# First batch of a four-stage transformer kernel: norms ahead of the weights' scaling, a second issuing queue for 12 of the head tiles' transfers

## The reference

```python
x = x + attn0(layernorm(x), W_kv, g_kv, W_kdec, W_vdec, W_q, W_qdec, W_krope, W_qrope, W_o)
# in attn0, for 16 heads
kv_c = rmsnorm(x @ W_kv) * g_kv          # 32 wide
q_c = x @ W_q                            # 64 wide
k = [kv_c @ W_kdec (8 a head), rope(x @ W_krope) (32 a head)]
q = [q_c @ W_qdec (8 a head), rope(q_c @ W_qrope) (32 a head)]
v = kv_c @ W_vdec
out = (softmax(causal(q k^T * scale)) v) @ W_o
```

## Time and profile before

| what | us |
|---|---|
| median of 3 runs | 1621.32 |
| lowest and highest run | 1618.19, 1621.41 |
| span of the profiled execution, first to last instruction | 1581.6 |
| median less span | 39.7 |

### The profile page before, as it was taken

The page is one execution under the profiler, slowest core; times in us unless marked ns, Lnnn a source line. Parts: engine busy times, 40 slices in busy tenths (PEclk is TensorE's granted clock), DMA queues, the critical chain, the costliest instruction groups (busy, mean ns, idle before and its releaser), DMA issues.

```text
span 1581.6 us, 37199 instructions
## 1 busy us (share of the span) xinstructions
PE 1288.0 (81%) x13212; PEld 843.4 (53%) x13212; DVE 1160.2 (73%) x3814; ACT 728.0 (46%) x1523; POOL 690.9 (44%) x1004
## 2 busy tenths in 40 slices
PE   4479899888899888989995799938998898666891
PEld 2244544445454454545544566627776776556780
DVE  4578787896988969888764554428889998973556
ACT  1145456555555555555560133424545444215773
POOL 3023232233332333324231122347878788764664
PEclk9689999999999999999995899968879678658996
DMA  3675726556175561745606111102111112032335
GB/s 104 88 113 78 116 34 105 78 92 111 26 116 79 93 104 26 122 79 92 101 9 225 38 34 33 40 22 83 44 43 44 50 50 71 21 118 77 99 92 169
DMA packets 73863, 123.19 MB, mean 78 GB/s; under 512 B 17518, under 2 KB 46067, under 8 KB 72784
## 3 DMA queue, kind: packets, MB, share of 16 engines
q1 hardware_dynamic: 64960, 106.74, 35.5%
q0 software_dynamic: 7616, 13.59, 2.6%
q10 hardware_dynamic: 1104, 0.48, 0.1%
HBM read 30.40 MB, written 17.60 MB: 30 GB/s over the span
## 4 chain that ended last, share of the span: by engine, by line
PE 39%; DVE 30%; POOL 10%; issue 8%; DMA 5%; SPq 4%; ACT 3%; DVEq 1%; POOLq 0%; ACTq 0%
DVE first L780 5%; PE A L594 5%; PE S L1034 5%; PE S L577 4%; DVE S L783 4%; PE S L566 4%; POOL xq L1357 3%; SPq L500 3%; DVE tA L759 2%; PE A L1046 2%; PE S L558 2%; DVE tB L760 2%; PE A L1996 2%; DMA Qp<-mT 2%; PE S L179 2%
## 5 line engine op out<-in xcount | busy, mean ns | idle before, releaser
L671 ACT ACTIVATE P<-S 128x512 f32<-128x512 f32 (+3 forms) x768 | 333.1, 491 | 281.5 <-PE S L577 277.2
L854 POOL TENSOR_SCALAR_AFFINE_SELECT P<-P 128x256 f32<-128x256 f32 (+1 forms) x256 | 116.8, 460 | 384.9 <-ACT P L671 384.7
L566 PE MATMUL S<-Kp,Qp 120*128 120x512 f32 (+3 forms) x768 | 251.5, 396 | 36.0 <-DMA Kp<-rck 18.6
L577 PE MATMUL S<-Qp,Kp 121*128 121x512 f32 (+3 forms) x768 | 251.6, 391 | 35.4 <-DVE tB L760 9.8
L783 DVE CUSTOM_DVE_ANT_0 S<-S,later 128x512 f32<-128x512 f32 (+3 forms) x512 | 239.2, 514 | 39.4 <-PE S L566 38.8
L566 PEld LDWEIGHTS S<-Kp,Qp 120*128 120x128 f32 x768 | 133.5, 195 | 168.7 <-issue 75.5
L780 DVE TENSOR_REDUCE first<-S 128x1 f32<-128x512 f32 x256 | 164.5, 684 | 49.5 <-PE S L566 49.2
L577 PEld LDWEIGHTS S<-Qp,Kp 121*128 121x128 f32 x768 | 138.2, 191 | 112.4 <-issue 24.0
L594 PE MATMUL A<-P,V 128*9 128x512 f32 (+3 forms) x1536 | 175.3, 505 | 5.0 <-POOL P L854 5.0
L2133 POOL DMA_INDIRECT yq<-yq,id x71 | 69.4, 978 | 46.2 <-DVE yq L2096 22.5
L1780 POOL TENSOR_TENSOR prod<-qf,kT 128x128 f32<-128x128 f32 x160 | 72.8, 488 | 34.7 <-ACT qf L1615 21.7
(11 more groups left out here) (335 smaller groups left out, 2696.2 us busy)
## 6 DMA issues: line engine op xcount, KB each, us to landing
Qp<-rcq SPq DMA_DIRECT2D x64, 256.0 KB
Kp<-rck SPq DMA_DIRECT2D x64, 256.0 KB
Qp<-rcq SPq DMA_DIRECT2D x64, 128.0 KB
Kp<-rck SPq DMA_DIRECT2D x64, 128.0 KB
xq<-xq SPq DMA_DIRECT2D x71, 72.0 KB, 1.9
yb<-yq SPq DMA_DIRECT2D x8, 528.0 KB, 7.1
Qp<-cq SPq DMA_DIRECT2D x64, 64.0 KB
Kp<-ck SPq DMA_DIRECT2D x64, 64.0 KB
```

Source lines behind the costliest of these rows:

```text
L566: te.matmul(S[s][:, 512 * h:512 * h + n], Q[0:120, h, 128 * qt:128 * qt + 128], K[0:120, h, 512 * part:512 * part + n], start=True, stop=T ...
L577: te.matmul(S[s][:, 512 * h + c:512 * h + 512], K[0:121, h, 128 * kb:128 * kb + 128], Q[0:121, h, 512 * qh + c:512 * qh + 512], start=True ...
L671: se.activation(k.P[(w.n - 1) % NP0][:, h, c:512], S[s][:, 512 * h + c:512 * h + 512], ACT.Exp, scale=SCALE0).then_inc(p.done("st").h, 1)
L854: ge.affine_select(P[:, :, start:c + 128], P[:, :, start:c + 128], [[0, 2], [1, wide]], ALU.is_ge, 0.0, base=start - c, channel_multiplier ...
```

## The change

1. DVE starts with the list at once. The wait for the weights and the two scalings come after `ln4` of batch 0.
2. x of batch 0 is loaded in two transfers of four tiles each, and `ln1` waits for both.
3. `wqT`, `wqr` and `wqd` get a semaphore of their own, `d_wf`, and `fuse` waits for that. The other five stay on `d_w`. `kv` and `wo` on TensorE now wait for `d_w`.
4. Of the shipping of units 0 and 1, 12 transfers move from SP's to ACT's queue: head 1 of K of unit 0, of Q of unit 1 and of K of unit 1. ACT issues them in one block after its copy for `v` of batch 0, behind waits for `v_rope_l` 4 and `done("ck")` 1. SP keeps head 0 of these three, both heads of Q of unit 0, and everything from unit 2 on.

```diff
--- before.py
+++ after.py
@@ -470,10 +470,19 @@
     return (k.P[4], k.P[5]) if w.n in (2, 4) else (k.tA, k.tB)
 
 
+def ship(k, u, name, high, dst, h):
+    r, q = 16 * (2 * u % 8 + h), 8 * (2 * u % 16 + h)
+    rope, content = k.RH[name][r:r + 16].bitcast(F32), k.CH[name][q:q + 8].bitcast(F32)
+    for at, many, src in ((64, 2, rope[:, high]), (96, 1, content[:, high:high + 1]), (104, 2, content),
+                          (0, 4, rope.rearrange("p a b t -> p (a b) t"))):
+        yield dst[at:at + many * src.shape[0], h, :].bitcast(F32), src
+
+
 def attn0_sync(p, k, sp, ye):
     a = p.a
     x_in = a["x"].rearrange("(n p) d -> p n d", p=128)
-    ye.dma_start(p.x[:, 0:8, :], x_in[:, 0:8, :]).then_inc(p.sem("d_x").h, 16)
+    for i in range(2):
+        ye.dma_start(p.x[:, 4 * i:4 * i + 4, :], x_in[:, 4 * i:4 * i + 4, :]).then_inc(p.sem("d_x").h, 16)
     for t, n in ((k.cos[:], "cos"), (k.sin[:], "sin"), (k.R["ck"][:], "wkr"), (k.later[:, 384:512], "mqk")):
         ye.dma_start(t, a[n]).then_inc(p.sem("d_c").h, 16)
     for b in range(1, B):
@@ -491,16 +500,12 @@
             else:
                 sp.wait_ge(p.sem("v_rope_l"), 2 if name == "cq" else 4)
             sp.wait_ge(p.done(name), b + 1)
-            for h in range(2):
-                r, q = 16 * (2 * u % 8 + h), 8 * (2 * u % 16 + h)
-                rope, content = k.RH[name][r:r + 16].bitcast(F32), k.CH[name][q:q + 8].bitcast(F32)
-                for at, many, src in ((64, 2, rope[:, high]), (96, 1, content[:, high:high + 1]), (104, 2, content),
-                                      (0, 4, rope.rearrange("p a b t -> p (a b) t"))):
-                    rows = dst[at:at + many * src.shape[0], h, :].bitcast(F32)
+            for h in range(1 if u == 1 or (u == 0 and name == "ck") else 2):
+                for rows, src in ship(k, u, name, high, dst, h):
                     ye.dma_start(rows, src).then_inc(p.sem(f"d_{name[1]}{u % 4}").h, 16)
 
 
-CONSTS0, WEIGHTS0 = 16 * 4, 16 * 8
+CONSTS0, WEIGHTS0 = 16 * 4, 16 * 5
 
 
 def attn0_tensor(p, k, pe, te):
@@ -516,11 +521,12 @@
             pe.wait_ge(p.sem("v_xn"), w.n)
             turn_over(te, p, S[s], k.xn, 8).then_inc(p.made("xnT").h, 1)
         elif w.kind == "fuse":
-            pe.wait_ge(p.sem("d_w"), WEIGHTS0)
+            pe.wait_ge(p.sem("d_wf"), 16 * 3)
             te.matmul(S[s][:, 0:512], k.wqT[:], k.P[0][0:64, 0, :], start=True, stop=True)
             te.matmul(S[s][:, 512:640], k.wqT[:], k.P[2][0:64, 0, 0:128], start=True, stop=True).then_inc(p.made("fuse").h, 1)
         elif w.kind == "kv":
             pe.wait_ge(p.done("xnT"), w.n)
+            pe.wait_ge(p.sem("d_w"), WEIGHTS0)
             for i in range(8):
                 ins = te.matmul(S[s][:, 32 * i:32 * i + 32], k.xnT[:, 128 * i:128 * i + 128], k.wkv[:], start=True, stop=True)
             ins.then_inc(p.made("kv").h, 1)
@@ -614,8 +621,9 @@
 def attn0_scalar(p, k, act, se):
     S, a = p.S, p.a
     se.dma_start(p.ident[:], a["ident"]).then_inc(p.sem("d_id").h, 16)
-    for t, n in ((k.wqT[:], "wqT"), (k.P[0][0:64, 0, :], "wqr"), (k.P[2][0:64, 0, 0:128], "wqd"), (k.wkv[:], "wkv"), (k.gkv[:], "gkv"),
-                 (k.W["wkd"][:], "wkd"), (k.W["wvd"][:], "wvd"), (k.W["wo0"][:], "wo0")):
+    for t, n in ((k.wqT[:], "wqT"), (k.P[0][0:64, 0, :], "wqr"), (k.P[2][0:64, 0, 0:128], "wqd")):
+        se.dma_start(t, a[n]).then_inc(p.sem("d_wf").h, 16)
+    for t, n in ((k.wkv[:], "wkv"), (k.gkv[:], "gkv"), (k.W["wkd"][:], "wkd"), (k.W["wvd"][:], "wvd"), (k.W["wo0"][:], "wo0")):
         se.dma_start(t, a[n]).then_inc(p.sem("d_w").h, 16)
     for w in k.items:
         s = w.slot
@@ -662,6 +670,12 @@
                 act.wait_ge(p.made("pv"), 48 * (w.n - 2))
             se.activation(k.V[(w.n - 1) % 2][:, :, :, 0:8], S[s][:].rearrange("p (n h d) -> p n h d", n=8, h=16),
                           ACT.Copy).then_inc(p.done("v").h, 1)
+            if w.n == 1:
+                act.wait_ge(p.sem("v_rope_l"), 4)
+                act.wait_ge(p.done("ck"), 1)
+                for u, name, tiles, high in ((0, "ck", k.K, 1), (1, "cq", k.Q, 0), (1, "ck", k.K, 1)):
+                    for rows, src in ship(k, u, name, high, tiles[u % 4], 1):
+                        se.dma_start(rows, src).then_inc(p.sem(f"d_{name[1]}{u % 4}").h, 16)
         elif w.kind == "st":
             c = w.at[3]
             if w.n > NP0:
@@ -689,9 +703,6 @@
     ve.memset(k.later[:, 0:384], 0.0)
     for A in p.A:
         ve.memset(A[:], 0.0).then_inc(p.sem("v_zero").h, 1)
-    dve.wait_ge(p.sem("d_w"), WEIGHTS0)
-    ve.tensor_scalar(k.W["wkd"][:], k.W["wkd"][:], k.gkv[:, 0:1], None, ALU.mult)
-    ve.tensor_scalar(k.W["wvd"][:], k.W["wvd"][:], k.gkv[:, 0:1], None, ALU.mult).then_inc(p.sem("v_weights").h, 1)
     for w in k.items:
         s = w.slot
         if w.kind in ("rn", "rl", "rhot", "rpos"):
@@ -703,7 +714,7 @@
             ln_stats(p, dve, ve, x[:, 8 * b + 4 * h:8 * b + 4 * h + 4, :], 4)
         elif w.kind == "ln1":
             b = w.at[0]
-            dve.wait_ge(p.sem("d_x" if b == 0 else "d_x2"), 16 if b == 0 else 16 * (B - 1))
+            dve.wait_ge(p.sem("d_x" if b == 0 else "d_x2"), 16 * 2 if b == 0 else 16 * (B - 1))
             ln_stats(p, dve, ve, x[:, 8 * b:8 * b + 8, :], 8)
         elif w.kind == "ln2":
             k.ln[w.at] = w.n
@@ -718,6 +729,10 @@
         elif w.kind == "ln4":
             b = w.at[0]
             ln_apply(p, ve, k.xn, x[:, 8 * b:8 * b + 8, :], range(4, 8)).then_inc(p.sem("v_xn").h, 1)
+            if b == 0:
+                dve.wait_ge(p.sem("d_w"), WEIGHTS0)
+                ve.tensor_scalar(k.W["wkd"][:], k.W["wkd"][:], k.gkv[:, 0:1], None, ALU.mult)
+                ve.tensor_scalar(k.W["wvd"][:], k.W["wvd"][:], k.gkv[:, 0:1], None, ALU.mult).then_inc(p.sem("v_weights").h, 1)
         elif w.kind == "kv2":
             dve.wait_ge(p.done("kv"), w.n)
             if w.n == 1:
```

## The result

The changed kernel took 1609.47 us, median of 12 runs, beside 1616.61 us for the kernel before, also 12 runs (its first three are the 1621.32 above). The ratio is 0.9953, 95% interval 0.9936 to 0.9970: **7.6 us faster, between 4.9 and 10.3**. Timed again in a later series it was 0.9939 (0.9912 to 0.9966). The interval lies wholly on the faster side, and the middle of it lies past the 0.2% that the prediction set.

The account below looks back on a forecast made before the run. Two bounds in a row were seen: a wait for weights, then the shipping stream. Head 4.4 + stream 3.3 + ACT's wait 1.6 = 9.3 us, so 1621.3 - 9.3 = 1612.0 us, range 1608 to 1618.

Parts of the forecast that it names:

- The head, 4.40 us: Norms ahead of the weight scaling: POOL's first operation starts at 10.65 instead of 15.05, worth 4.40 us, not 7.1.
- rival B: In the head: DVE's statistics stretch POOL's clearing, at most 2.3 us less gain; 1614.3 with the higher rate; chance 0.13.
- The fused weight: TensorE's fuse in the head: its own semaphore lets it end at 11.9; worth 0 to 0.3 us, taken as 0.
- The split of x: Loading of x in the head: two transfers cost one more SP issue, 0.44 us, within 2.7 us of slack; worth nothing.
- The chain to the key shipping moves as a whole: PE, ACT and DVE work up to the key shipping moves together, from 56.16 to 51.8 us.
- The 1 us allowed for the clock: TensorE's clock steps may fall elsewhere: up to 2.7 us either way, mostly beside DVE, so 1 us allowed.
- The stream's rate, 1.5 times: Shipping on SP and ACT queues: rate 1.5 times as high while both are full; about 3.3 us at unit 0's keys.
- maxima near 60.5: Sign in the changed profile: DVE's maxima start near 60.5 us with the higher shipping rate, near 63 with an unchanged one.
- rival A: In the shipping: the stream keeps its rate, gains are 4.4 + 1.0, ACT's 2.66 us wait stays; 1615.9 us; chance 0.25.
- ACT's wait, 1.6 us: ACT's 2.66 us wait for unit 3's shipped queries goes; worth between 1.4 and 2.66 us, taken as 1.6.
- Rival C: In the shipping: uneven queue shares delay ACT's 12 transfers to 92.2 us; 4.9 us slower, 1626.2; chance 0.04.
- The 39.7 us outside the span: Whole kernel: median 1621.32 us against a profiled span of 1581.6; the 39.7 us between were taken as unchanged.

Follow-up runs that it names:

- the two partial kernels: The changed kernel with all shipping back on SP, ratio 0.9977; and the kernel before with only the 12 transfers on ACT's queue, ratio 0.9985.
- two runs above: The changed kernel with x in one transfer (1570.68 us, 0.991 of the kernel before), and with fuse waiting for all eight weights (no time given).

## Why the prediction was right, and where not

**The head, 4.40 us: right**, 4.34 measured. That POOL would be late next was right too: of the 7.4 us by which the statistics moved, 3.1 were lost on its clears, and the run with the clears cut in two got 2.9 of them back. Nothing happened to the clears beside the statistics (rival B). The fused weight was put at 0 to 0.3 us and is worth 0.4; `wqd` landed at 10.1, not 9.4. The split of x is worth nothing, as said.

**The chain to the key shipping moves as a whole: right** where the clock step falls alike (4.31 us). The 1 us allowed for the clock was too little: one step is worth up to 3, and the changed kernel itself showed both.

**The stream's rate, 1.5 times: wrong.** The step that failed is "a second queue of packets beside the first should pass some of the time", worked out from 156 against 365 GB/s per whole share. That comparison was sound in saying that something other than the engines holds the packets. It did not say that a second queue gets around it, and the run with other source partitions shows what does. Nor did it help that heads 0 and 1 come from different partitions, which the prediction held to speak for the higher rate. The measured factor is 136 / 122 = 1.11 (137 / 119 = 1.15 in the two partial kernels, both on one chip). Unit 0's keys gained 0.35 us where 3.3 stood in the sum, unit 1's 2.2 where 8 stood. By the prediction's own sign, maxima near 60.5 or, with rival A, near 63, the measured 63.44 speaks for A.

**ACT's wait, 1.6 us: about right.** It went, and from the first exponential to ACT's copy the lead grew from 5.59 to 6.94, by 1.35. But it went for a smaller reason than forecast: unit 3's last query transfer was issued at 96.02 instead of 103.72, 3.4 us ahead of the common shift and not 8. The margin was thin, since in two runs above ACT waited there again.

**The sum.** By the events 4.3 + 0.35 + 0.9 (unit 1's keys holding TensorE for 1.19 us instead of 3.07, and what that is worth at the first exponential) + 1.35 = 6.9 us, where the forecast had 9.3 and rival A, the stream unchanged, 5.4. The truth lies between them, and the measured 7.6 (4.9 to 10.3) can't tell which is nearer: the interval takes in both. That 1609.47 lies within 2.5 us of 1612.0 is partly luck: the kernel before came down by 4.7 (from 1621.32 to 1616.61 with more runs), and the medians moved by 7.1 instead of 9.3, which works the other way. The term for the stream was wrong by nearly all of its 3.3 us at unit 0's keys; that the events fall short by 2.4 us and not by 3 is owed to unit 1's keys, which gave 0.9 that the sum did not have as a term. Rival C did not happen: SP's 12 transfers were issued by 71.3 us, ACT's by 72.9, so the shares were even. **The 39.7 us outside the span were read wrongly.** They are 1.8 in the changed kernel, and the profiled execution of the kernel before came, by all signs, from a faster chip (last section). It cost nothing, since only differences were summed.

## What to carry to other kernels

When a first step is moved forward, look for the in-order engine that comes next and what stands in front of its part: here clears on GpSimd took 3 of 7 us, and moving them had to respect that they stop VectorE where both want SBUF. When a stream of transfers is slow, ask what its packets have in common before adding a queue: spreading the source over more partitions gave 1.35 to 1.4 times the rate, a second queue 1.11 to 1.15. With a few microseconds in 1600, read events from the span's start, and only between points that TensorE's clock step doesn't lie between.

## What the runs showed of the hardware

The chips differ in a place far from the change. In the last stage SP issues eight transfers whose address it loads from a tile first. In the kernel with the clears cut in two, on two chips, SP's timeline reads:

```profile
1412.07 8.86 SPq L1947 DMA_DIRECT2D xq<-pads  x8
```

```profile
1416.07 20.91 SPq L1947 DMA_DIRECT2D xq<-pads  x8
```

The 71 expert tiles behind them ran from 1432.5 to 1534.6 us on the one and from 1440.9 to 1557.2 on the other. The kernel before took 1585.15 us on the first chip and 1618.29 on the second (1618.09 on a third). By its 8.21 us for the eight transfers and its span, its profile above was of the first kind; its three runs, 1618.19 to 1621.41, fit the second. So a kernel's time is only to be set against runs on the same chip. Which part of these transfers is slow was not tried.
